# Moving ScalarE's division and beta k copy ahead of the silus of q and k in the first stage

## The chip, the core and the metric

The kernel runs on one NeuronCore of a Trainium2 chip. The metric is the device time of one execution in microseconds (us). The engines of the core are TensorE (PE in the profile; PEld is its weight load), VectorE (DVE), ScalarE (ACT), GpSimd (POOL) and SyncE (SP), which issues the DMAs. Each works through its own list of instructions in order and waits on semaphores for the others.

## The reference, cut to what matters

There are 32 samples of 750 x 256. Every second row is kept (384 tokens in three blocks of 128, the last padded), each block attends to itself, and a gated delta-rule attention and a mixture of six experts follow. Only the front of the second layer is touched by the change:

```python
h = _L0_tok_ref(x)                          # blockwise softmax attention
h = h + _L0_attn_ref(_layernorm(h), ...)
h = h + _L0_ffn_ref(_layernorm(h), ...)
# inside _L0_attn_ref
q = silu(causal_dwconv(x @ Wq, conv_q_w))   # 4 taps; k and v alike
beta = sigmoid(x @ Wb)
q = l2norm(q); k = l2norm(k)                # needs the sums of q*q and k*k by head
kb = k * beta[..., None]
A = tril(einsum('bhnid,bhnjd->bhnij', kbc, kc), -1)
```

All data is float32.

## The kernel before

The kernel has three stages. The first one, in `first_phase`, loads the samples and leaves q, k, v, beta k and the triangular systems in packs in DRAM. It is software-pipelined: each call of `body` works on three samples at once. For sample a it does the block attention and the layer norm statistics, for sample b the projections to q, k and v, the causal convolution and the silus of q and k, and for sample c the silu of v, the norms by head, the short filter, beta k and the product k (beta k). Every engine has a `body` of its own in which the calls for a, b and c are interleaved by hand, and that written order is the order in which the engine works. One turn of `body` is called a period below. There are 30 turns that hold all three samples, and a few at both ends that hold fewer.

The parts that the prediction follows, with the lines of the profile:

- TensorE: `attend` (L409) multiplies the probabilities by x and signals `attn_ready`. `transpose_kb` (L465) follows, then `project(b, ..., 5)` (L431, the last of six projections: two for q, two for k, two for v), then `k_kb` (L481, 96 small products of k and beta k, waiting for both halves of beta k). The next turn begins with `transpose_normed` (L417, waits for the normalised rows xn), `head_values` (L444, 36 matmuls of 128 columns; it waits for the squares of q and k through `sq_ready`), projections 0 and 1 (L431, waiting for both copies of the transposed xn) and `transpose_head_values` (L451).
- ScalarE: a tap of the convolution for each projection (`last_tap`, L579), the copy of the transposed probabilities and other copies (L541), the division of the attention rows by their sums (`divide_attn`, L563, three blocks), the silus (L588) and the squares SQ (L638). Silu and exp lie in different table sets, so each turn has two loads of a table (ACT_TABLE_LOAD), one at the first silu of q and one at the exp of beta (L573).
- VectorE: the other three taps of the convolution (L703), the copy of the second half of beta k (L775), the layer norm statistics (L670 to L676), the normalisation (L682, xn), the mask of the systems (L737), the second copy of the transposed xn (L687) and the short filter (L724, L728), which waits for the silus of v.
- GpSimd: the power that gives one over the standard deviation (L797), between L676 and L682.

The queue of SyncE stores the packs and loads the next sample in the same order of samples.

Of the kernel before, what the change touches and what calls it, by code (L numbers as in the profile page):

```python
# [146 lines left out]
def first_phase(nc, x, w, shared, v_all):  # L147

    NB, dram, bank, ident, upper, expanded = (shared[k] for k in ("NB", "dram", "bank", "ident", "upper", "expanded"))
    with ExitStack() as c:  # L150
# [5 lines left out]
        def signal(name, per=1, primed=1):  # L156
            signals.append(Signal(c.enter_context(nc.semaphore(name)), per, primed))
            return signals[-1]
# [38 lines left out]
        def field(buf, at):  # L197
            return buf[:, at:at + HALF * T]

        def chans(buf, at):  # L200
            return field(buf, at).rearrange("p (a t) -> p a t", a=HALF)

        def toks(buf, at):
            return field(buf, at).rearrange("p (b c) -> p b c", b=BLK)
# [3 lines left out]
        pack_stored = [signal(f"pack_stored{s}", 16) for s in range(2)]  # L208
# [57 lines left out]
        with nc.Block() as block:  # L266
            @block.vector
            def _(dve):
                dve.memset(wb[:, :, :], 0.0).then_inc(started, 1)
                dve.memset(headsel[:, :, :], 0.0).then_inc(started, 1)  # L270
                dve.wait_ge(started, 2)
                for n in range(2 * HALF):
                    for head in range(2):
                        dve.memset(headsel[head * DH:(head + 1) * DH, n, 2 * n + head:2 * n + head + 1], 1.0).then_inc(started, 1)
                dve.memset(minus_half[:, :], -0.5).then_inc(started, 1)
                for q in range(NQ):
                    dve.tensor_copy(strict[q * SC:(q + 1) * SC, :],
                                    upper[q * SC:(q + 1) * SC, P + q * SC:P + (q + 1) * SC]).then_inc(started, 1)
                dve.wait_ge(started, 11 + NQ)
# [30 lines left out]
        with nc.Block() as block:  # L310
# [227 lines left out]
            @block.scalar  # L538
            def _(act):
                def copy(dst, src):  # L540
                    return act.activation(dst, src, ACT.Copy)  # L541

                def copy_xT(n):
                    act.wait_ge(*xT_ready.now(n, 1))
                    copy(xT[:, 0:2, :, :].rearrange("p b a t -> p (b a t)"), bank[0][:, :]).then_inc(xT01_copied.sem, 1)

                def exp_scores(n):
                    act.wait_ge(*negmax_ready.now(n))
                    for b in range(BLK):
                        act.activation(E[:, b, :], bank[2][:, b * P:(b + 1) * P], ACT.Exp, bias=negmax[:, b:b + 1],  # L550
                                       scale=float(D) ** -0.5, accum_out=rs[:, b:b + 1]).then_inc(probs_ready.sem, 1)

                def copy_probsT(n):
                    act.wait_ge(*probsT_ready.now(n))
                    copy(PT[:, :, :].rearrange("p b t -> p (b t)"), bank[1][:, 0:T]).then_inc(probsT_copied.sem, 1)

                def divide_attn(n, s, pair):
                    H = toks(pb[s], HF)
                    act.wait_ge(*attn_ready.now(n))
                    act.wait_ge(*rinv_ready.now(n))  # L560
                    act.wait_ge(*h_stored[s].before(pair))
                    for b in range(BLK):
                        act.activation(H[:, b, :], attn_bank[b // 2][:, (b % 2) * D:(b % 2 + 1) * D], ACT.Copy,  # L563
                                       scale=rinv[:, b:b + 1]).then_inc(h_ready.sem, 1)

                def copy_xnT(n, s):
                    act.wait_ge(*xnT_ready.now(n, 1))
                    copy(chans(pb[s], XNT)[:, 0, :], bank[1][:, 0:T]).then_inc(xnT0_copied.sem, 1)

                def exp_beta(n):  # L570
                    act.wait_ge(*hvk_ready.now(n))
                    act.wait_ge(*beta_step.before(n))
                    act.activation(eb[:, :].rearrange("p (b h) -> p b h", b=BLK),  # L573
                                   hvk[:, :, 2 * NH:],
                                   ACT.Exp, scale=-1.0).then_inc(eb_ready.sem, 1)

                def last_tap(it, j):
                    act.wait_ge(*proj_ready.now(it, j + 1))
                    act.activation(Y[:, j, :], proj_bank[j][:, 0:T], ACT.Copy, scale=convw[:, j, CK - 1:CK])\  # L579
                        .then_inc(tap_done.sem, 1)  # L580

                def silu(it, s, j):
                    dst = (chans(pa[s], QT), chans(pa[s], KT), VT)[j // 2]
                    act.wait_ge(*conv_step.now(it, 6 * (j // 2) + 5 + j % 2))
                    if j == 4:
                        act.wait_ge(*fir_step.before(it))
                        act.wait_ge(*vtok_ready.before(it))
                    act.activation(dst[:, j % 2, :], Y[:, j, :], ACT.Silu).then_inc(silu_done.sem, 1)  # L588

                def body(a=None, b=None, c=None, s=0, apair=None, bpair=None):  # L590
                    if b is not None:
                        copy_xnT(b, 1 - s)
                    if c is not None:
                        silu(c, s, 4)
                        silu(c, s, 5)
                        act.wait_ge(*hv_ready.now(c))
                        copy(HVT[:, :], bank[6][0:BLK * SC, 0:P]).then_inc(hv_copied.sem, 1)
                    if b is not None:
                        last_tap(b, 0)
                        last_tap(b, 1)  # L600
                    if a is not None:
                        copy_xT(a)
                    if c is not None:
                        exp_beta(c)
                        act.wait_ge(*ktok_ready.now(c))
                        copy(field(pa[s], KTOK)[:, 0:2 * D], bank[6][:, :])
                        copy(field(pa[s], KTOK)[:, 2 * D:], bank[7][:, 0:D]).then_inc(ktok_copied.sem, 1)
                    if b is not None:
                        last_tap(b, 2)
                    if a is not None:  # L610
                        exp_scores(a)
                    if b is not None:
                        last_tap(b, 3)
                    if a is not None:
                        copy_probsT(a)
                    if c is not None:
                        act.wait_ge(*fs_ready.now(c))
                        act.wait_ge(*fs_stored.before(c))
                        copy(fsk[:, 0:2 * D], bank[6][:, :])
                        copy(fsk[:, 2 * D:], bank[7][:, 0:D]).then_inc(fs_copied.sem, 1)  # L620
                    if b is not None:
                        last_tap(b, 4)
                        act.wait_ge(*pack_stored[1 - s].before(bpair))
                        silu(b, 1 - s, 0)
                        silu(b, 1 - s, 1)
                    if a is not None:
                        divide_attn(a, s, apair)
                    if c is not None:
                        act.wait_ge(*kbT_ready.now(c, 1))
                        copy(chans(pa[s], KBT)[:, 0, :], bank[6][:, 0:T]).then_inc(kbT0_copied.sem, 1)  # L630
                    if b is not None:
                        silu(b, 1 - s, 2)
                        last_tap(b, 5)
                        silu(b, 1 - s, 3)
                        act.wait_ge(*silu_done.now(b, 4))
                        act.wait_ge(*ssq_ready.before(b))
                        for f in range(2):
                            act.activation(SQ[:, 2 * f:2 * f + 2, :].rearrange("p a t -> p (a t)"),  # L638
                                           field(pa[1 - s], (QT, KT)[f]), ACT.Square).then_inc(sq_ready.sem, 1)

                body(a=0, s=0, apair=0)
                body(a=1, b=0, s=1, apair=0, bpair=0)
                for i in range(0, NB // 2 - 1):
                    body(2 * i + 2, 2 * i + 1, 2 * i, 0, i + 1, i)
                    body(2 * i + 3, 2 * i + 2, 2 * i + 1, 1, i + 1, i + 1)
                body(b=NB - 1, c=NB - 2, s=0, bpair=NB // 2 - 1)
                body(c=NB - 1, s=1)
# [1471 lines left out]
```

## Time and profile before

| | us |
|---|---|
| median of 3 runs | 2776.16 |
| lowest, highest | 2775.27, 2777.48 |
| the profiled execution: device time | 2788.52 |
| the profiled execution: span of the trace | 2786.8 |
| first stage in the trace | about 0 to 770 |
| busy in the whole span: TensorE, VectorE, ScalarE, GpSimd | 2513.8, 1924.8, 1377.7, 537.1 |
| mean granted TensorE clock, share of full | 0.911 |

Times in the trace are read from the start of the span. A row of the view in order of time gives the start, the length, the engine, the line, the operation with output <- inputs, the shape and how many instructions are merged in it; behind it in brackets stands the time that the engine idled ahead of it and what ended that. The granted clock (PEclk) is 1.00 at 2.4 GHz and 0.50 at 1.2 GHz.

### The profile page before, as it was taken

The numbers are of one execution on the slowest core, as the hardware profiler recorded it, in microseconds if no ns is written. First come the engines' busy times: TensorE is split into PE (matmuls) and PEld (weight loads), VectorE is DVE, ScalarE is ACT, GpSimd is POOL, SyncE is SP. The second block draws the span as 40 slices with busy tenths as digits, with TensorE's granted clock in tenths as the row PEclk, the third lists the DMA queues.
The fourth block names the chain that finished last, engine by engine and source line by source line (L and its number), as shares of the span: only waits on it lengthen the run. The fifth ranks groups of instructions, "written<-read, shape, count | busy, mean of one in ns | idle before, by whom it ended". The sixth has DMA issues, their size and how long they took to land.

```text
span 2786.8 us, 53423 instructions
## 1 busy us (share of the span) xinstructions
PE 2513.8 (90%) x21052; PEld 1899.8 (68%) x21052; DVE 1924.8 (69%) x5233; ACT 1377.7 (49%) x2633; POOL 537.1 (19%) x373
## 2 busy tenths in 40 slices
PE   5888888888698789999999999999999999999997
PEld 3666666666477667777777777767777777677765
DVE  4888988898778245676667766776676566656655
ACT  3777777777533224444444454444444444444442
POOL 1333333333300011111111111111111111111110
PEclk9999999999896569999999999999899999999998
DMA  2666666666688411132123212221222122212200
GB/s 76 196 202 200 221 203 198 207 208 196 204 326 335 155 58 55 66 109 66 61 75 123 66 61 79 96 66 61 87 88 89 61 93 81 66 61 91 81 18 18
DMA packets 223161, 334.47 MB, mean 120 GB/s; under 512 B 113856, under 2 KB 190624, under 8 KB 213696
## 3 DMA queue, kind: packets, MB, share of 16 engines
q1 hardware_dynamic: 219744, 309.03, 33.6%
q10 hardware_dynamic: 2304, 12.58, 1.1%
q0 software_dynamic: 864, 9.44, 0.8%
q8 instruction: 168, 2.75, 0.4%
q14 instruction: 81, 0.66, 0.1%
HBM read 191.68 MB, written 164.23 MB: 128 GB/s over the span
## 4 chain that ended last, share of the span: by engine, by line
PE 49%; DVE 9%; ACT 6%; issue 3%; DVEq 0%
PE bank L1527 8%; PE bank L1537 8%; PE bank L1470 5%; PE bank L1365 4%; PE bank L1481 3%; PE bank L1499 3%; PE bank L1448 3%; ACT L1674 3%; PE bank L1433 2%; PE bank L1474 2%; PE bank L1396 2%; PE bank L1404 2%; DVE DL L1869 2%; DVE v_all L1955 1%; ACT HE L1674 1%
## 5 line engine op out<-in xcount | busy, mean ns | idle before, releaser
L1537 PE MATMUL bank<-w2e,HE 128*128 128x256 f32 x1152 | 312.4, 411 | 11.8 <-DVE v_all L1955 8.9
L1955 DVE SCALAR_TENSOR_TENSOR v_all<-bank,we,v_all 128x256 f32<-128x256 f32 x576 | 242.9, 477 | 111.1 <-PE bank L1537 108.8
L703 DVE SCALAR_TENSOR_TENSOR Y<-bank,convw,Y 128x383 f32<-128x383 f32 (+2 forms) x576 | 314.6, 606 | 5.9 <-ACT Y L579 5.9
L1527 PE MATMUL bank<-v_all,w1e 128*128 128x384 f32 x768 | 313.6, 535 | 1.3 <-ACT HE L1674 1.3
L431 PE MATMUL bank<-pb,wqkv 128*128 128x384 f32 x768 | 285.8, 503 | 6.6 <-issue 6.4
L1537 PEld LDWEIGHTS bank<-w2e,HE 128*128 128x128 f32 x1152 | 221.2, 203 | 53.5 <-issue 16.2
L1835 DVE TENSOR_TENSOR L<-bank,b2g 128x48 f32<-128x48 f32 x32 | 6.6, 207 | 342.3 <-PE bank L1481 342.3
L1674 ACT ACTIVATE HE<-bank 128x384 f32<-128x384 f32 x192 | 94.1, 490 | 222.4 <-PE bank L1527 221.7
L1470 PE MATMUL bank<-v_all,w1g 128*128 128x384 f32 x512 | 201.8, 517 | 0.4 <-ACT v_all L1666 0.4
L1527 PEld LDWEIGHTS bank<-v_all,w1e 128*128 128x128 f32 x768 | 146.7, 208 | 72.6 <-issue 23.3
L431 PEld LDWEIGHTS bank<-pb,wqkv 128*128 128x128 f32 x768 | 138.1, 197 | 79.9 <-issue 21.8
L803 POOL TENSOR_TENSOR RR<-RS,minus_half 128x24 f32<-128x24 f32 x32 | 133.2, 4163 | 273.8 <-DVE RS L752 273.8
L1657 ACT ACTIVATE v_all<-bank 128x192 f32<-128x192 f32 x192 | 60.2, 331 | 247.5 <-DVE v_all L1773 247.4
L2074 POOL TENSOR_TENSOR v_all<-v_all,WT 128x768 f32<-128x768 f32 x32 | 72.5, 2266 | 538.2 <-DVE WT L1854 538.2
L579 ACT ACTIVATE Y<-bank,convw 128x384 f32<-128x384 f32 x192 | 112.0, 584 | 77.1 <-PE bank L431 76.0
L2080 POOL TENSOR_TENSOR m<-m,minus_half_q 128x12 f32<-128x12 f32 x32 | 72.6, 2268 | 375.0 <-DVE m L1875 375.0
L1649 ACT ACTIVATE first_stage<-bank 32x384 f32<-32x384 f32 (+1 forms) x192 | 89.0, 479 | 98.8 <-PE bank L1385 43.1
L1448 PEld LDWEIGHTS bank<-W,v_all 128*128 128x128 f32 x768 | 107.6, 212 | 36.6 <-ACT W L1649 25.7
L1448 PE MATMUL bank<-W,v_all 128*128 128x64 f32 x768 | 113.6, 296 | 15.0 <-ACT W L1649 15.0
L1365 PE MATMUL bank<-v_all 64*128 64x256 f32 x768 | 116.4, 424 | 11.5 <-PEq L918 5.5
L1674 ACT ACT_TABLE_LOAD x93 | 119.3, 1283 | 1.8
L1470 PEld LDWEIGHTS bank<-v_all,w1g 128*128 128x128 f32 x512 | 87.9, 191 | 43.0 <-issue 1.2
(211 smaller groups left out, 5431.0 us busy)
## 6 DMA issues: line engine op xcount, KB each, us to landing
packa<-pa SPq DMA_DIRECT2D x32, 1932.0 KB, 8.1
v_all<-packa SPq DMA_DIRECT2D x32, 1932.0 KB, 7.7
packb<-pb SPq DMA_DIRECT2D x32, 768.0 KB, 6.1
v_all<-packb SPq DMA_DIRECT2D x32, 768.0 KB, 7.0
toeplitz<-taps SPq DMA_DIRECT2D x128, 190.0 KB, 5.1
toep<-toeplitz SPq DMA_DIRECT2D x32, 760.0 KB, 8.6
packb<-fsk SPq DMA_DIRECT2D x32, 384.0 KB, 2.3
first_stage<-fl SPq DMA_DIRECT2D x32, 384.0 KB, 5.4
```

Source lines behind the costliest of these rows:

```text
L431: mm = pe.matmul(proj_bank[j][:, 0:T], wqkv[:, a, j * P:(j + 1) * P], xnT[:, a, :], start=(a == 0), stop=(a == HALF - 1))
L579: act.activation(Y[:, j, :], proj_bank[j][:, 0:T], ACT.Copy, scale=convw[:, j, CK - 1:CK])\
L703: dve.scalar_tensor_tensor(out=Y[:, j, lag:T], in0=proj_bank[j][:, 0:T - lag], scalar=convw[:, j, CK - 1 - lag:CK - lag], in1=Y[:, j, lag: ...
L803: pool.tensor_tensor(RR[:, :, :, :].rearrange("p b n h -> p (b n h)"), RS[:, :], minus_half[:, :], ALU.pow)\
L1365: mm = pe.matmul(bank[odd][:, hh * 2 * P:(hh + 1) * 2 * P], kT[rows, hh, pair * P:(pair + 1) * P], qkb[rows, :, hh, pair * P:(pair + 1) * ...
L1448: mm = pe.matmul(bank[1][:, h * DH:(h + 1) * DH], ATM[:, even_heads_first(b, h), 0:P], W[:, h, :], start=(b == 0 and h == 0), stop=True, s ...
L1470: pe.matmul(mlp_bank[m][:, 0:T], w1g[:, a, m * P:(m + 1) * P], chans(pb[s], PX)[:, a, :], start=(a == 0), stop=False)
L1527: mm = pe.matmul(bank[6][:, 0:T], w1e[:, a, k, :], YT[s][:, a, :], start=(a == 0), stop=(a == HALF - 1))
L1537: mm = pe.matmul(expert_bank(b), HE[k % 2][:, b * P:(b + 1) * P], w2e[:, k, :], start=True, stop=True)
L1649: return act.activation(dst, src, ACT.Copy)
L1674: act.activation(HE[k % 2][:, :], bank[6][:, 0:T], ACT.Gelu_apprx_tanh).then_inc(he_ready.sem, 1)
L1955: dve.scalar_tensor_tensor(out=HA[s][:, b, :], in0=expert_bank(b), scalar=we[s][:, b, k:k + 1], in1=HA[s][:, b, :], op0=ALU.mult, op1=ALU. ...
```

## The change

In ScalarE's `body`, the silus of the two halves of q (`silu(b, 1 - s, 0)` and `1`) and the wait for the stored pack move behind the division of the attention rows of sample a and the copy of the first half of beta k of sample c. The last tap of the sixth projection (`last_tap(b, 5)`) moves ahead of all four silus. The number of instructions and of table loads stays the same.

```diff
                     if b is not None:
                         last_tap(b, 4)
-                        act.wait_ge(*pack_stored[1 - s].before(bpair))
-                        silu(b, 1 - s, 0)
-                        silu(b, 1 - s, 1)
                     if a is not None:
                         divide_attn(a, s, apair)
                     if c is not None:
                         act.wait_ge(*kbT_ready.now(c, 1))
                         copy(chans(pa[s], KBT)[:, 0, :], bank[6][:, 0:T]).then_inc(kbT0_copied.sem, 1)
                     if b is not None:
+                        last_tap(b, 5)
+                        act.wait_ge(*pack_stored[1 - s].before(bpair))
+                        silu(b, 1 - s, 0)
+                        silu(b, 1 - s, 1)
                         silu(b, 1 - s, 2)
-                        last_tap(b, 5)
                         silu(b, 1 - s, 3)
```

The lists of TensorE, VectorE, GpSimd and SyncE are the same in both programs. On ScalarE, in a turn with all three samples, from the tap of the fifth projection (L579, the row ahead of the table load) to the squares, there stands before:

```order
L579 ACTIVATE Y<-bank,convw 128x384
L588 ACT_TABLE_LOAD
L588 ACTIVATE pa<-Y 128x384 x2
L563 ACTIVATE pb<-bank,s 128x256 x3
L541 ACTIVATE pa<-bank 128x384
L588 ACTIVATE pa<-Y 128x384
L579 ACTIVATE Y<-bank,convw 128x384
L588 ACTIVATE pa<-Y 128x384
L638 ACTIVATE SQ<-pa 128x768 x2
```

and now:

```order
L579 ACTIVATE Y<-bank,convw 128x384
L563 ACTIVATE pb<-bank,s 128x256 x3
L541 ACTIVATE pa<-bank 128x384
L579 ACTIVATE Y<-bank,convw 128x384
L588 ACT_TABLE_LOAD
L588 ACTIVATE pa<-Y 128x384 x4
L638 ACTIVATE SQ<-pa 128x768 x2
```

The table load stands three kinds of work later, behind the division (L563), the copy of beta k (L541) and the tap of the sixth projection, and the four silus stand together between it and the squares.

On ScalarE in the last turn that has a sample b, and no sample a any more, there stands before, from the last copy of the short filter's rows on:

```order
L541 ACTIVATE fsk<-bank 128x256
L579 ACTIVATE Y<-bank,convw 128x384
L588 ACT_TABLE_LOAD
L588 ACTIVATE pa<-Y 128x384 x2
L541 ACTIVATE pa<-bank 128x384
L588 ACTIVATE pa<-Y 128x384
L579 ACTIVATE Y<-bank,convw 128x384
L588 ACTIVATE pa<-Y 128x384
L638 ACTIVATE SQ<-pa 128x768 x2
L588 ACTIVATE VT<-Y 128x384 x2
```

and now:

```order
L541 ACTIVATE fsk<-bank 128x256
L579 ACTIVATE Y<-bank,convw 128x384
L541 ACTIVATE pa<-bank 128x384
L579 ACTIVATE Y<-bank,convw 128x384
L588 ACT_TABLE_LOAD
L588 ACTIVATE pa<-Y 128x384 x4
L638 ACTIVATE SQ<-pa 128x768 x2
L588 ACTIVATE VT<-Y 128x384 x2
```

Here too the load stands behind the copy of beta k and the tap of the sixth projection.

## Rows read from the trace of the kernel before

**Rows 1.** Stretch: busy PE PEld DVE ACT POOL, PEclk, DMA, GB/s; four periods between silu table loads.
```profile
339.41:362.65 23.24, 20.38 (x216) 14.94 (x215) 19.58 (x52) 16.47 (x35) 8.05 (x7) 0.85 0.62 195
362.65:384.60 21.95, 19.05 (x216) 14.23 (x215) 19.63 (x52) 16.48 (x36) 8.05 (x7) 0.92 0.66 208
384.60:406.02 21.42, 17.75 (x216) 13.19 (x215) 19.57 (x52) 16.35 (x35) 8.04 (x7) 1.00 0.65 212
406.02:428.21 22.19, 19.34 (x216) 14.22 (x215) 19.62 (x52) 16.47 (x35) 8.11 (x8) 0.92 0.63 205
```

**Rows 2.** TensorE in order of time, in the period without low clock.
```profile
383.80 1.46 PE L409 MATMUL bank<-x,PT 128*128 128x256 f32 x6
...
385.75 1.46 PE L431 MATMUL bank<-pb,wqkv 128*128 128x384 f32 x4
388.39 1.01 PE L481 MATMUL bank<-pa 64*32 64x32 f32 x96 [1.19 <-issue]
391.07 0.88 PE L417 MATMUL bank<-ident,xn 128*128 128x128 f32 x6 [1.67 <-DVE xn L682]
391.88 1.07 PE L444 MATMUL bank<-SQ,headsel 128*32 128x128 f32 x24
392.78 0.61 PE L444 MATMUL bank<-pb,wb 128*32 128x128 f32 x12
394.20 2.82 PE L431 MATMUL bank<-pb,wqkv 128*128 128x384 f32 x8 [0.81 <-issue]
```

**Rows 3.** ScalarE in order of time, in the same period.
```profile
384.00 0.58 ACT L579 ACTIVATE Y<-bank,convw 128x384 f32<-128x384 f32 x1
384.60 1.28 ACT L588 ACT_TABLE_LOAD   x1
385.89 0.94 ACT L588 ACTIVATE pa<-Y 128x384 f32<-128x384 f32 x2
386.73 1.18 ACT L563 ACTIVATE pb<-bank,s 128x256 f32<-128x256 f32 x3
387.80 0.50 ACT L541 ACTIVATE pa<-bank 128x384 f32<-128x384 f32 x1
...
388.58 0.59 ACT L579 ACTIVATE Y<-bank,convw 128x384 f32<-128x384 f32 x1
389.05 0.54 ACT L588 ACTIVATE pa<-Y 128x384 f32<-128x384 f32 x1
389.62 1.58 ACT L638 ACTIVATE SQ<-pa 128x768 f32<-128x768 f32 x2
```

**Rows 4.** VectorE in order of time, in the same period.
```profile
385.95 0.56 DVE L775 COPY pa<-bank 128x384 f32<-128x384 f32 x1 [0.64 <-PE bank L465]
387.22 1.16 DVE L670 BATCH_NORM_STATS2 st<-pb 128x6 f32<-128x256 f32 x3 [0.72 <-ACT pb L563]
...
389.96 1.06 DVE L682 TENSOR_SCALAR xn<-pb,mv,s 128x256 f32<-128x256 f32 x3
...
393.56 0.55 DVE L687 COPY pb<-bank 128x384 f32<-128x384 f32 x1
```

**Rows 5.** TensorE in order of time, in the last turn with a sample b.
```profile
745.03 1.07 PE L444 MATMUL bank<-SQ,headsel 128*32 128x128 f32 x24 [1.84 <-ACT SQ L638]
```

**Rows 6.** TensorE in order of time, in the period with 6.83 us at low clock.
```profile
347.36 1.93 PE L444 MATMUL bank<-SQ,headsel 128*32 128x128 f32 x24
...
350.07 3.58 PE L431 MATMUL bank<-pb,wqkv 128*128 128x384 f32 x8
```

**Rows 7.** The same view as rows 1, the stretches at low clock.
```profile
344.74:351.57 6.83, 5.68 (x45) 4.13 (x46) 6.70 (x17) 3.08 (x6) 0.00 (x0) 0.50 0.91 300
368.63:372.05 3.42, 2.88 (x27) 2.42 (x30) 3.42 (x9) 1.91 (x4) 0.00 (x0) 0.50 0.91 364
...
413.00:416.42 3.42, 3.42 (x41) 2.48 (x40) 3.30 (x8) 1.59 (x4) 0.00 (x0) 0.50 0.89 274
```

**Rows 8.** Silu's table load in the first stage: count, length, first and last start.
```profile
L588 ACT ACT_TABLE_LOAD  x30: 1283/1283/1283, 73.1 to 719.1; - x30
```

## The prediction

> **What bounds the kernel now.** I read the busy times by period first. All 30 full turns lie between the silu table loads from 73.1 to 719.1 us [rows 8], so a period is (719.1 - 73.1) / 29 = 22.28 us. The four shown come in turn: 23.24, 21.95, 21.42 and 22.19 us, at a mean granted clock of 0.85, 0.92, 1.00 and 0.92 [rows 1]. The order of instructions is the same in all four, and ScalarE and VectorE are busy for the same time in each; only TensorE's clock differs. So the period has two parts: a base of 21.42 us at full clock, and what the low clock adds.
>
> The base is read from the orders in time of the period at full clock. Zero is 384.60, where the table load starts [rows 3]. TensorE has three gaps: 1.19 us ahead of the products of k and beta k, 1.67 us ahead of the transposes of xn (VectorE), and 0.81 us ahead of projection 0 [rows 2], which starts when VectorE has copied its half of the transposed xn at 393.56 + 0.55 = 394.11 [rows 4]. Elsewhere it runs through. The first gap waits for ScalarE's copy of beta k, which ends at 388.30 [rows 3]; the second is the chain division, statistics, xn, in which VectorE idles 0.72 us for ScalarE's division [rows 4]. That is what the change goes for.
>
> **The low clock.** It is granted at 344.74 for 6.83 us, at 368.63 for 3.42 us, not at all in the third period, and at 413.00 for 3.42 us [rows 1, 7]. Against the zero of its own period it starts at +5.33, +5.98 and +6.98. All three starts lie behind the first gaps of TensorE. In the stretch of 6.83 us TensorE was idle for 6.83 - 5.68 = 1.15 us before it ran on; in the two of 3.42 us for 0.54 us and not at all [rows 7].
>
> **The change, on ScalarE.** The attention product ends at 383.80 + 1.46 = 385.26 [rows 2]. ScalarE is free at 384.60, and now waits 0.70 us, which the table load used to fill. Then, with the distances of start to start in [rows 3]:
> - division at 385.30, not 386.73;
> - copy of beta k 1.07 later, at 386.37, done at 386.87, not 388.30;
> - tap of the sixth projection, which ends at 385.75 + 1.46 = 387.21 [rows 2]: at 387.26, not 388.58. ScalarE waits 0.5 us here as well;
> - table load 0.60 later, at 387.86; first silu 1.29 later, at 389.15; the fourth three times 0.42 later, at 390.41 (0.84 for two); squares 0.57 later, at 390.98, not 389.62; done at 392.56, not 391.20.
>
> **On VectorE.** Its copy of beta k stays at 385.95 to 386.51, since that waits for TensorE. The statistics start at 386.53 instead of 387.22, 0.69 us earlier, and the chain through GpSimd to xn moves by the same, so xn starts at 389.27 instead of 389.96 [rows 4]. The second copy of the transposed xn then ends near 393.42 instead of 394.11. The short filter, next, waits for the silus of v, which ScalarE ends near 394.0; it stays within the slack that projection 0 leaves.
>
> **On TensorE.** The products of k and beta k start at 387.25: the gap of 1.19 us is gone. They take 1.01 us, and then it waits until 391.07 - 0.69 = 390.38 for the transposes of xn: a gap of 2.1 us instead of 1.67. Those end at about 391.2. Then comes what is new: head_values needs the squares, and starts at 392.56 + 0.05 = 392.61 instead of 391.88, after a gap of 1.4 us. That it can wait for them the last turn shows, where TensorE idles 1.84 us for the squares already [rows 5]. From 391.88 to 393.39 less the 0.07 by which neighbouring groups overlap it takes 1.44 us [rows 2], so projection 0 starts at 394.05 instead of 394.20. The rest of the turn is TensorE's own as before. The base becomes 21.42 - 0.15 = 21.27 us: of 1.4 us gained at the division, 0.15 is left, since the squares are 1.36 us later.
>
> **What the clock adds now.** Before, 0.81 us of slack ahead of projection 0 swallowed part of each low stretch. Now head_values has none behind it. At low clock it takes 350.07 - 347.36 = 2.71 us [rows 6] instead of 1.44: +1.27. Eight matmuls of projection took 3.58 us with the first 1.50 us at low clock, against 2.82: 0.76 lost, half the low time [rows 2, 6, 7]. In the changed period head_values starts at +8.01 (392.61) and ends at +10.72 at low clock. A low stretch of 6.83 us that starts at +X therefore costs 1.27 + (X + 6.83 - 10.72) / 2.
>
> Which stretch comes is the choice on which the forecast rests. TensorE is idle from +3.7 to +5.8 and from +6.6 to +8.0, with 0.8 us of transposes between. I take it that the clock falls in every period, since the two gaps together (3.5 us) are nearly as long as the three of before (3.67 us) but stand closer, and that it stays low for 6.83 us: the second gap, 1.4 us, lies in the first part of a stretch that begins between +5.3 and +6.6, as the 1.15 us did in the long stretch of before. For X the rows give a hint. After the period of 23.24 us with the long stretch the next start came 5.98 - 5.33 = 0.65 us later in its period [rows 1, 7]; a period of 23.24 + 0.65 = 23.89 us would find it in the same place. X = 6.6 gives 1.27 + 1.36 = 2.63 and 21.27 + 2.63 = 23.90 us, so this place reproduces itself: a start earlier than that makes the period shorter and moves the next start later. The bounds are X = 5.3 (+1.98, period 23.25) and X = 7.1 (+2.88, 24.15).
>
> **The sum.** 29 periods x (23.90 - 22.28) = +47.0 us; about -1 until the start has settled; in the last turn TensorE waits for the squares already, so their 1.4 us come on top: +47. With the bounds +28 and +54. The second and third stage have the same instructions. The trace has 2786.8 us of span in 2788.52 of device time; I add the difference to the median: 2776.2 + 47 = 2823 us. Its own range is 2804 to 2832.
>
> **A rule of the skill.** The rows show low clock after gaps of 1.19 and 1.67 us [rows 2, 7]. The Trainium skill, page "TensorE: Matmul & The Clock Gate", section "HAM oscillation — how this bites in real kernels", tells of a loop whose matmuls wait for a DMA in each K-tile, 3 to 5 us long, and that paid the low clock in every turn. If only gaps that long cost the clock, this kernel's would be free and the result that of rival three; the rows contradict that, as three of four periods pay.
>
> **Rivals.**
> One, a short stretch in each period: after the fall the clock is full again 3.42 us later. It would start between +7.3 and +8.9, and cost 1.27 to 1.66, so 22.5 to 22.9 us a period: +8 to +20 us, 2784 to 2796. For it speaks that two of three stretches of before were short; against it the second gap.
> Two, the pattern of before stays (5.33 long, 5.98 short, none, 6.98 short). Then the four periods are 23.26, 21.92, 21.27 and 22.40, with 1.38 and 2.41 us of head_values at low clock at 1.27 / 2.71 each. They sum to 88.85 against 88.80: no change, 2776 to 2780. Against it: one of the four now has a gap of 1.4 us where it had none.
> Three, faster: TensorE's first gap is closed, and if that is what let the clock fall, no period has a low stretch. Then 29 x (21.27 - 22.28) = -29 us, 2749. The point is whether 2.1 us and 1.4 us of idleness with work between keep the clock; the third period had 1.67 and 0.81 and kept it. I hold it for unlikely, as the gaps grow.
> Four, the low stretch grows longer than 6.83 us, or the squares are later than worked out (another 0.5 us a period is +15 us): 2835 to 2860.
> That the change doesn't act can be left out: the division did wait behind the load [rows 3].
>
> **Chances.** The forecast 0.55, rival one 0.17, two 0.12, three 0.08, four 0.08. A measurement of this kernel can tell 0.2% (5.6 us) from no change, so slower is 0.80, same 0.12, faster 0.08. The range leaves out rival three and most of two and four: 2778 to 2836 us.
>
> **What would show it.** In the trace after: division about 1.4 us earlier against the tap ahead of it; TensorE's gap ahead of the products of k and beta k gone, that ahead of the transposes of xn near 2.1 us, and a wait of head_values for the squares of about 1.4 us in nearly every turn; a period of 23.9 us with a mean clock of (23.9 - 3.42) / 23.9 = 0.86 against 0.92 now. If head_values does not wait for the squares, the step on ScalarE is wrong; if the base at full clock is not near 21.3, the path; if base and gaps are right and the period isn't, the clock.

## The result and the profile after

The changed kernel takes 2828.88 us (median of 4 runs, 2824.33 to 2839.04) against 2776.82 us (2775.27 to 2779.96) before: a ratio of 1.0191, with a 95% interval of 1.0162 to 1.022. It is slower by 52 us, 1.9%, clear of the noise. The prediction said 2823.

Two turns of the changed kernel in the view of busy time by stretch, from silu table load to load, and the low stretches of three turns with the full one between them; columns as in [rows 1]:

```profile
410.24:434.13 23.89, 20.36 (x237) 14.73 (x227) 19.41 (x52) 16.37 (x36) 8.05 (x6) 0.86 0.58 190
434.13:458.02 23.89, 20.36 (x237) 14.72 (x226) 19.41 (x53) 16.37 (x35) 8.06 (x6) 0.86 0.59 191
437.51:444.34 6.83, 5.50 (x41) 3.67 (x42) 4.86 (x10) 2.76 (x6) 0.00 (x0) 0.50 0.88 232
444.34:461.40 17.06, 14.87 (x175) 11.05 (x173) 14.55 (x42) 13.61 (x30) 8.06 (x6) 1.00 0.47 175
461.40:468.23 6.83, 5.49 (x41) 3.67 (x42) 4.86 (x10) 2.76 (x6) 0.00 (x0) 0.50 0.82 221
```

These answer [rows 1] and [rows 7]. The four different periods of before (23.24, 21.95, 21.42, 22.19 us) have become one, 23.89 us, with a low stretch (half clock, PEclk 0.50) of 6.83 us in each. The table loads, by count, length, first and last start:

```profile
L588 ACT ACT_TABLE_LOAD  x30: 1283/1283/1283, 76.5 to 768.6; - x30
```

(768.6 - 76.5) / 29 = 23.87 us against 22.28 [rows 8]. TensorE in order of time through one turn; it answers [rows 2] and [rows 6]:

```profile
432.03 1.46 PE L431 MATMUL bank<-pb,wqkv 128*128 128x384 f32 x4
433.42 1.02 PE L481 MATMUL bank<-pa 64*32 64x32 f32 x96
436.48 0.87 PE L417 MATMUL bank<-ident,xn 128*128 128x128 f32 x6 [2.04 <-DVE xn L682]
438.84 1.93 PE L444 MATMUL bank<-SQ,headsel 128*32 128x128 f32 x24 [1.49 <-ACT SQ L638]
440.55 1.07 PE L444 MATMUL bank<-pb,wb 128*32 128x128 f32 x12
441.55 4.22 PE L431 MATMUL bank<-pb,wqkv 128*128 128x384 f32 x8
```

The gap ahead of the products of k and beta k (L481) is gone. The one ahead of the transposes of xn has grown from 1.67 to 2.04 us, and head_values (L444) now waits 1.49 us for the squares. It then runs at low clock for 441.55 - 438.84 = 2.71 us, and the eight matmuls of projection behind it take 4.22 us instead of 2.82. ScalarE and VectorE in order of time in the same turn, which answer [rows 3] and [rows 4]:

```profile
431.58 1.20 ACT L563 ACTIVATE pb<-bank,s 128x256 f32<-128x256 f32 x3 [0.71 <-PE bank L409]
432.67 0.50 ACT L541 ACTIVATE pa<-bank 128x384 f32<-128x384 f32 x1
433.53 0.58 ACT L579 ACTIVATE Y<-bank,convw 128x384 f32<-128x384 f32 x1 [0.36 <-PE bank L431]
434.13 1.28 ACT L588 ACT_TABLE_LOAD   x1
435.42 1.76 ACT L588 ACTIVATE pa<-Y 128x384 f32<-128x384 f32 x4
437.22 1.58 ACT L638 ACTIVATE SQ<-pa 128x768 f32<-128x768 f32 x2
```
```profile
432.71 1.07 DVE L670 BATCH_NORM_STATS2 st<-pb 128x6 f32<-128x256 f32 x3
435.37 1.06 DVE L682 TENSOR_SCALAR xn<-pb,mv,s 128x256 f32<-128x256 f32 x3
438.96 0.55 DVE L687 COPY pb<-bank 128x384 f32<-128x384 f32 x1
440.03 0.75 DVE L724 TENSOR_SCALAR fsT<-VT,firw 128x384 f32<-128x384 f32 x2 [0.52 <-ACT VT L588]
```

ScalarE idles 0.71 us for the attention product and 0.36 us for the sixth projection, time in which the table load and silus used to run. VectorE no longer waits for the division. Its statistics follow its copy of beta k at once.

### The profile page after: what moved, and what is told of

Same layout as the page of the kernel before. It is cut to its first block, busy times and chain, and to the rows that moved or that the text cites. A ratio compares the mean times of both kernels' runs of the same rounds, so it can differ in the third digit from the quotient of the medians.

```text
span 2828.5 us, 53423 instructions
## 1 busy us (share of the span) xinstructions
PE 2538.6 (90%) x21052; PEld 1904.4 (67%) x21052; DVE 1920.4 (68%) x5233; ACT 1375.9 (49%) x2633; POOL 537.5 (19%) x373
## 4 chain that ended last, share of the span: by engine, by line
PE 46%; DVE 11%; ACT 6%; issue 3%; DVEq 0%
PE bank L1537 8%; PE bank L1527 7%; PE bank L1470 5%; PE bank L1365 4%; PE bank L1481 3%; PE bank L1499 3%; ACT L1674 3%; PE bank L1448 2%; PE bank L1474 2%; PE bank L1433 2%; DVE DL L1869 2%; PE bank L1396 2%; PE bank L1404 2%; DVE v_all L1955 2%; ACT HE L1674 1%
## 5 line engine op out<-in xcount | busy, mean ns | idle before, releaser
L431 PE MATMUL bank<-pb,wqkv 128*128 128x384 f32 x768 | 320.3, 553 | 0.9 <-issue 0.7
L431 PEld LDWEIGHTS bank<-pb,wqkv 128*128 128x128 f32 x768 | 154.9, 220 | 94.2 <-issue 49.9
L579 ACT ACTIVATE Y<-bank,convw 128x384 f32<-128x384 f32 x192 | 111.8, 582 | 122.4 <-PE bank L431 121.2
```

What stands on the lines that cost most here:

```text
L431: mm = pe.matmul(proj_bank[j][:, 0:T], wqkv[:, a, j * P:(j + 1) * P], xnT[:, a, :], start=(a == 0), stop=(a == HALF - 1))
```

## The experiments

In every kernel below "period" is the distance of the silu table loads: last start less first start, by 29. Ratios are to the kernel before in the same set of runs.

### Filling the gaps, first size (e1, e2)

To tell a loss by the clock from a loss by the wait, the order is left alone and TensorE is given work in its gaps. The work is without use and its result is overwritten; such matmuls are called fillers below. The clock theory says that the 52 us are the low clock; the path rival says that they are the new wait of TensorE for the squares.

```diff
+                def fill(n, k):
+                    for _ in range(n):
+                        pe.matmul(bank[k][:, 0:P], ident[:, :], ident[:, :], start=True, stop=True, skip_group_check=True)
...
+                        fill(14, 1)             # e1; e2: fill(11, 1)
                         transpose_normed(b)
...
+                        pe.wait_ge(*at_copied.before(c))
+                        fill(9, 6)              # e1 alone
                         head_values(c, s)
...
+                        fill(8, 1)              # e2 alone
                         k_kb(c, s)
```

> The changed kernel, with idle TensorE time filled: in each full turn 14 matmuls of the identity by itself (128 columns, about 0.13 us each) ahead of the wait for xn, and 9 ahead of the wait for the squares, into banks that are free there; their results are overwritten. Clock theory (the loss is the low clock that every turn takes on behind the gaps, the path itself is about 0.1 us a turn shorter than before): no low stretch is left in the full turns, the period is 21.3 us, the time 2748 us (2742 to 2756). Path rival (the loss is the wait for the squares itself): the fillers only sit in gaps, the period stays at 23.9 us and the time near 2829 us. If only one of the gaps matters, something between.

> The kernel before, with 8 such matmuls ahead of the products of k and beta k and 11 ahead of the wait for xn. Clock theory: no low stretch, every period as the one at full clock, 21.4 us, so 2776 - 29 x 0.86 = 2751 us. Path rival: 2776 us. The difference to the filled changed kernel is the path alone: clock theory says that kernel is the faster one by 2 to 5 us, path rival slower by some 50.

Measured: e1 2796.13 us, ratio 1.0065 (1.0042 to 1.0088), period 22.78 us; e2 2770.68 us, ratio 0.9966 (0.9945 to 0.9987), period 21.87 us. Neither theory's number came. Busy time by stretch of e1, and its fillers on TensorE in order of time:

```profile
300.00:500.00 200.00, 200.00 (x2318) 162.15 (x2317) 169.93 (x445) 143.74 (x304) 69.51 (x51) 1.00 0.63 205
```
```profile
394.25 3.39 PE L489 MATMUL bank<-ident 128*128 128x128 f32 x28
397.48 0.82 PE L417 MATMUL bank<-ident,xn 128*128 128x128 f32 x6
398.14 2.17 PE L489 MATMUL bank<-ident 128*128 128x128 f32 x18
400.24 1.07 PE L444 MATMUL bank<-SQ,headsel 128*32 128x128 f32 x24
```

### Filling the gaps, right size (e5, e6, e8, e11)

The same edit with 8 and 5 fillers in the changed kernel (e5), 4 and 6 in the kernel before (e6), and in the changed kernel one gap alone: 8 fillers ahead of xn (e8), 5 ahead of the squares (e11).

> The changed kernel with shorter fillers: 8 matmuls of the identity ahead of the wait for xn and 5 ahead of the wait for the squares. One takes 0.23 us in the trace of e1, so they make 1.9 and 1.2 us and fit into the gaps of 2.04 and 1.49 us, where those of e1 (3.2 and 2.1 us) were longer than the gaps. Clock theory: full clock in every turn, period 21.3 us, 2776 - 29 x 1.0 = 2747 us, give or take 8 for the later stages. Path rival: not below 2776, since the changed path has a wait more.

> The kernel before with fillers that fit its gaps: 4 (0.9 us) ahead of the products of k and beta k, 6 (1.4 us) ahead of the wait for xn. Clock theory: every turn as the one at full clock, 21.42 us, 2776 - 29 x 0.86 = 2751 us, give or take 8; e5 is then 0.15 us a turn, 4 us, faster than this. Path rival: e5 is the slower of the two.

> The changed kernel with the gap ahead of xn filled alone (8 fillers), that of 1.4 us ahead of the squares left. If the gap ahead of xn lets the clock fall and the second only keeps it low, every turn is at full clock and the period 21.3 us, 2747 us. If the gap for the squares is enough by itself, there are low stretches in some or all turns and the time lies between 2760 and 2829 us.

> The changed kernel with only the gap ahead of the squares filled (5 fillers), that of 2.04 us ahead of xn left. If the gap ahead of xn lets the clock fall and the gap for the squares keeps it low, there are low stretches again but only short ones (3.4 us): 21.3 to 22.6 us a turn, 2750 to 2785 us. If the gap ahead of xn keeps the clock low by itself, the period stays at 23.9 us and the time at 2829 us.

| kernel | median us | ratio (95%) | period us |
|---|---|---|---|
| e5 changed, both gaps | 2756.48 | 0.9907 (0.9881 to 0.9932) | 21.26 |
| e6 before, both gaps | 2757.27 | 0.9922 (0.9899 to 0.9945) | 21.45 |
| e8 changed, gap ahead of xn alone | 2748.78 | 0.9889 (0.9861 to 0.9916) | 21.26 |
| e11 changed, gap ahead of the squares alone | 2765.58 | 0.9942 (0.9925 to 0.996) | 21.66 |

Table loads of e5, e6, e8 and e11, in that order:

```profile
L597 ACT ACT_TABLE_LOAD  x30: 1283/1283/1283, 75.3 to 691.9; - x30
```
```profile
L596 ACT ACT_TABLE_LOAD  x30: 1283/1283/1283, 73.0 to 695.1; - x30
```
```profile
L594 ACT ACT_TABLE_LOAD  x30: 1283/1283/1283, 76.2 to 692.6; - x30
```
```profile
L595 ACT ACT_TABLE_LOAD  x30: 1283/1283/1283, 77.4 to 705.6; - x30
```

The stretch from 300 to 500 us of e8, and TensorE in one of its turns:

```profile
300.00:500.00 200.00, 186.12 (x2125) 142.36 (x2124) 182.73 (x481) 154.06 (x335) 78.23 (x59) 1.00 0.65 211
```
```profile
397.39 0.87 PE L417 MATMUL bank<-ident,xn 128*128 128x128 f32 x6
399.76 1.07 PE L444 MATMUL bank<-SQ,headsel 128*32 128x128 f32 x24 [1.50 <-ACT SQ L644]
```

Here the wait for the squares is whole, 1.50 us, the clock is full, and the period is 21.26 us, 1.0 us less than the 22.28 of the kernel before, and 0.19 less than that kernel with its own gaps filled (e6). So the wait alone costs nothing net: the changed path is the shorter one. What costs is the clock: with the gap of 2.04 us ahead of xn filled, there is no low stretch in any full turn (nor in those of e5 and e6). With only the other filled (e11), every second or third turn has a low stretch, and it is short. The turn of e11 that holds one, the inner part of the stretch, and the full clock behind it until after the next load; then TensorE in that turn:

```profile
402.02:424.43 22.41, 20.37 (x248) 15.64 (x237) 19.42 (x53) 16.38 (x35) 8.06 (x6) 0.92 0.61 204
405.60:408.80 3.20, 3.20 (x34) 2.80 (x36) 2.69 (x7) 2.29 (x5) 0.00 (x0) 0.50 0.84 205
409.00:427.80 18.80, 16.76 (x193) 12.45 (x188) 16.32 (x46) 13.88 (x31) 8.06 (x6) 1.00 0.55 196
```
```profile
404.37 0.88 PE L417 MATMUL bank<-ident,xn 128*128 128x128 f32 x6 [2.04 <-DVE xn L689]
405.09 1.96 PE L489 MATMUL bank<-ident 128*128 128x128 f32 x10
406.98 1.93 PE L444 MATMUL bank<-SQ,headsel 128*32 128x128 f32 x24
```

TensorE goes from the transposes to head_values without a wait, and the clock is back after some 3.4 us. So the gap ahead of xn can bring the low clock by itself, in 10 of the 29 periods of e11, the gap of 1.5 us for the squares by itself does not (e8), and the long stretch in every turn came only with both.

The medians of e5, e6 and e8 differ less clearly than the periods. e5 and e8 have the same first stage and stand 8 us apart, which lies in the later stages and between executions. e5 came 1.5 us above its range of 2739 to 2755, and its median is only 0.8 us below that of e6 where 4 us were expected, which the noise hides. So both medians refute the path rival, which wanted e5 not below 2776, but that the changed path is shorter rests on the periods, 21.26 against 21.45 us.

### More work, same period (e3, e9)

Two fillers are added where TensorE runs without a gap, to the changed kernel (e3) and to the kernel before (e9):

```diff
                     pe.wait_ge(*xnT1_copied.before(n))
+                    fill(2, 0)
                     for b in range(BLK):
                         for a in range(HALF):
```

> The changed kernel with 2 more matmuls of 128 columns (0.27 us) in each turn ahead of the transposes of x, where TensorE runs without a gap and sets the pace. Self-reproducing theory: the period stays at 23.89 us, since the low stretch begins some 0.5 us earlier in its turn and costs 0.27 us less: 2829 us, within 3. Additive rival: 31 x 0.27 = 8 us more, 2837 us, low stretches in place.

> The kernel before with 2 more matmuls of 128 columns in each turn ahead of the transposes of x (0.47 us a turn, at the 0.23 us that one took in e1). Self-reproducing theory: 21.43 + 0.47 = 21.9 us at full clock; the long low stretch of before, starting at +5.3 to +5.7, cost 1.8 to 1.95 us, and 21.9 + 1.95 comes near 23.89 us, so the turns fall into step with the low stretch and stay there: 23.9 us a turn, 2776 + 47 = 2823 us, for 14 us of added work. Additive rival: 2776 + 14 = 2790 us, with the four alternating periods each 0.47 us longer.

Measured: e3 2829.49 us, ratio 1.0186 (1.013 to 1.0241), against 2828.88 for the changed kernel without them. At 0.23 us each the two add 0.47 us a turn, not 0.27, so the additive rival should have given 14 us. e9: 2828.44 us, ratio 1.0162 (1.0099 to 1.0225), 47 us for some 14 us of work. One turn of e3 and a part of its low stretch, then the same of e9:

```profile
438.20:462.09 23.89, 20.97 (x242) 15.45 (x231) 19.40 (x53) 16.43 (x35) 8.05 (x6) 0.86 0.57 192
440.80:447.40 6.60, 5.72 (x45) 4.10 (x44) 5.63 (x12) 3.51 (x8) 0.00 (x0) 0.50 0.81 240
```
```profile
494.69:518.58 23.89, 21.03 (x220) 15.54 (x219) 19.58 (x52) 16.53 (x35) 8.04 (x7) 0.86 0.59 190
500.60:507.20 6.60, 6.03 (x45) 4.43 (x46) 6.46 (x15) 2.50 (x5) 0.00 (x0) 0.50 0.85 272
```

In e3 the low stretch begins 440.7 - 438.2 = 2.5 us after the table load, where in the changed kernel it is 437.51 - 434.13 = 3.38 us. It begins some 0.9 us earlier in its turn, and with half the low time lost that gives back the 0.47 us. So a later low stretch costs more and an earlier one less, and the turn settles where both agree.

The changed kernel itself shows how. The first of its 29 periods and the low stretch in it:

```profile
76.51:100.02 23.51, 20.43 (x238) 14.82 (x228) 19.41 (x53) 16.38 (x36) 8.07 (x6) 0.85 0.60 194
79.11:85.94 6.83, 5.79 (x45) 3.95 (x44) 5.63 (x12) 3.51 (x8) 0.00 (x0) 0.50 0.93 269
```

The next long stretch starts at 103.00, 23.89 us after this one, though the period took 23.51. The same distance stands in the kernel before, 368.63 - 344.74, across a period of 23.24 us [rows 7]. A period that is shorter than 23.89 us therefore finds the next stretch later in its turn by what is missing, and half of that is added to the next period. The first periods are 23.51, 23.70, 23.79, 23.85 and 23.87 us: what is missing to 23.89 halves each time. Why long stretches stand 23.89 us apart, no run here shows.

e9 has the order of before, without the change, and reaches the same 23.89 us. It did not do so at once: its first eight periods varied between 21.9 and 24.8 us, so that its mean is 23.52, and its runs spread from 2804 to 2843.

### One part undone (e4)

The tap of the sixth projection goes back between the third and fourth silu; division and copy of beta k stay ahead.

```diff
-                        last_tap(b, 5)
                         act.wait_ge(*pack_stored[1 - s].before(bpair))
                         silu(b, 1 - s, 0)
                         silu(b, 1 - s, 1)
                         silu(b, 1 - s, 2)
+                        last_tap(b, 5)
                         silu(b, 1 - s, 3)
```

> The changed kernel with one part undone: the tap of the sixth projection stands between the third and fourth silu as before; division and copy of beta k stay ahead of the silus. The squares end 0.66 us earlier than in the changed kernel, but VectorE's first taps of v wait for the late tap, and xn and the second copy of the transposed xn come 1.1 us later: base 21.8 us, the gap ahead of the transposes of xn 3.2 us. Clock theory: one low stretch in every turn, period 22.6 to 23.9 us, 2786 to 2823 us, and no wait for the squares. Path rival (the wait for the squares is the loss): the time falls to that of before or below, 2770 to 2785 us.

Measured: 2831.9 us, ratio 1.0187 (1.0141 to 1.0234); period 23.84 us, and 23.89 a turn once settled, with the time 9 us above the range I gave. TensorE in order of time:

```profile
433.10 1.02 PE L481 MATMUL bank<-pa 64*32 64x32 f32 x96
437.64 1.54 PE L417 MATMUL bank<-ident,xn 128*128 128x128 f32 x6 [3.52 <-DVE xn L682]
439.11 1.93 PE L444 MATMUL bank<-SQ,headsel 128*32 128x128 f32 x24
```

There is no wait for the squares, and the kernel is as slow. The two waits are one wait of 3.52 us now, and the low stretch is again 6.83 us in every settled turn. This speaks against the path rival a second time, though less than e8 does, since TensorE idles as long in sum as before (3.53 us). It also shows that the long stretch does not need a second gap: one gap of 3.52 us brings it too.

### One silu ahead of the division (e7, e10)

The table load can fill ScalarE's wait for the attention product without holding up the division, if only one silu goes with it.

```diff
                         last_tap(b, 4)
+                        act.wait_ge(*pack_stored[1 - s].before(bpair))
+                        silu(b, 1 - s, 0)
                     if a is not None:
                         divide_attn(a, s, apair)
...
                         last_tap(b, 5)
-                        act.wait_ge(*pack_stored[1 - s].before(bpair))
-                        silu(b, 1 - s, 0)
                         silu(b, 1 - s, 1)
```

e10 is this alone; e7 has 2 fillers ahead of the products of k and beta k and 6 ahead of the transposes of xn besides.

> An order between the two: one silu of q stays ahead of the division, so that the table load fills ScalarE's wait for the attention product; the other three stand behind the tap of the sixth projection as in the changed kernel; 2 and 6 fillers ahead of the products of k and beta k and of the wait for xn. From the same rows: division 1.71 us after the fifth tap (2.13 before, 0.70 in the changed kernel), squares done at 6.61 (6.60, 7.96), xn 0.42 us earlier than before, no wait for the squares, projection 0 at 9.18 instead of 9.60: period 21.0 us, 2776 - 29 x 1.28 = 2739 us, give or take 8. If something else sets the pace at full clock, the period is 21.3 or more and the time 2747 or more.

> The order of e7 (one silu of q ahead of the division, three behind the tap of the sixth projection) without fillers. At full clock 21.02 us a turn (e7), with gaps of 0.7, 1.75 and 0.9 us. 23.89 us is out of reach: the long stretch would have to cost 2.87 us. So low stretches come in some turns as in the kernel before: 21.5 to 22.2 us a turn, 2754 to 2774 us. Rival (any ordering that is faster at full clock falls into step at 23.89 us as the changed kernel did): 2823 us or more.

Measured: e7 2741.32 us, ratio 0.986 (0.9833 to 0.9886), period 21.03 us; e10 2757.92 us, ratio 0.9916 (0.9884 to 0.9948), period 21.34 us, a little below the range of 21.5 to 22.2, while the time is within its range. Table loads and a stretch of e7, then of e10:

```profile
L596 ACT ACT_TABLE_LOAD  x30: 1283/1283/1283, 71.1 to 681.0; - x30
300.00:500.00 200.00, 188.01 (x2248) 145.05 (x2245) 186.23 (x486) 156.57 (x333) 76.43 (x59) 1.00 0.66 217
```
```profile
L588 ACT ACT_TABLE_LOAD  x30: 1283/1283/1283, 73.9 to 692.7; - x30
300.00:500.00 200.00, 172.21 (x1982) 128.28 (x1982) 185.16 (x482) 155.31 (x333) 79.58 (x59) 0.98 0.66 214
```

Both beat the two kernels. e10 does it by order alone: more than half of its turns take 21.02 us, and the others, most of them with a short low stretch of 3.4 us, 21.5 to 22.1. So a path that is faster at full clock need not fall into step. The expectation gives a reason, that a long stretch would have to cost 2.87 us to reach 23.89; that this is what keeps e10 out is argued and not tested.

## Why the prediction was right, point by point

- **ScalarE's chain.** The forecast counts from where the table load stood before, 0.60 us behind the start of the fifth tap. In the trace after, the tap of the next turn starts at 454.18, so that point is 454.78, and a turn of 23.89 us earlier 430.89. The division starts at +0.69, the load at +3.24 (forecast 3.26), the squares end at 437.22 + 1.58 = 438.80, +7.91 (7.96).
- **VectorE's chain.** xn starts at +4.48; forecast 389.27 - 384.60 = +4.67. The statistics start at +1.82 (forecast +1.93) and take 1.07 us where they took 1.16 while the division gated them. The forecast was 0.2 us late here, and for the turn it does not matter, since TensorE waits for the squares behind it.
- **TensorE's gaps.** Forecast: none, 2.1 and 1.4 us. Measured: none, 2.04 and 1.49.
- **The base at full clock.** Forecast 21.27 us; e5 and e8 show 21.26, and e6 shows 21.45 for the order before, where the prediction had read 21.42. The path gained 0.19 us a turn, about what was said (0.15).
- **The low clock.** A stretch of 6.83 us in every turn was the choice on which the forecast rested. It starts at 437.51 - 430.89 = +6.62; the forecast was +6.6. head_values takes 2.71 us in it, as taken over from [rows 6], and the turn is 23.89 us against 23.90. The reason given for the place, that a start earlier than that makes the turn shorter and moves the next start later, is what e3 and the first periods of the changed kernel show. The first low stretch starts at 79.11, which is 79.11 - (76.51 - 3.24) = +5.84, and the rule of the prediction gives 21.26 + 1.27 + (5.84 + 6.83 - 10.72) / 2 = 23.51 us, the measured period. The reason given for the length, the second gap, fits e11, which takes that gap away; e4 shows that one longer gap does the same. That the clock falls in every turn was taken from the sum of the gaps. It came so, but no run tests that reason by itself, and the prediction gave its whole forecast only 0.55.
- **The sum.** 29 x (23.87 - 22.28) = 46.1 us, against 47 - 1. What was mis-sized is the end of the stage. The sum put 1.4 us there. The last transposes of head values (L451) came 798.79 - 747.08 = 51.7 us later than before. Measured from the point where the table load stood before, 0.2 us of this lies ahead of the 29 periods and 5.4 us behind them. About 2.5 us of the 5.4 is the thirtieth turn with its low stretch, which a sum over 29 distances leaves out. The other 2.9 us is the last turn: head_values starts 1.9 us later in it, as the squares keep TensorE 4.40 us instead of 1.84 [rows 5] and only a part of that was won ahead of them, and a low stretch that begins at 795.94, behind this gap, makes head_values and what follows up to L451 take 3.08 us instead of 2.05.

ScalarE's fifth tap in the turn behind the one shown; TensorE in the last turns of the changed kernel, with the low stretch there; and the row of the kernel before that answers TensorE's last one:

```profile
454.18 0.58 ACT L579 ACTIVATE Y<-bank,convw 128x384 f32<-128x384 f32 x1
```
```profile
780.12 0.25 PE L451 MATMUL bank<-ident,HVT 96*128 96x96 f32 x1
...
795.71 1.76 PE L444 MATMUL bank<-SQ,headsel 128*32 128x128 f32 x24 [4.40 <-ACT SQ L638]
...
798.79 0.39 PE L451 MATMUL bank<-ident,HVT 96*128 96x96 f32 x1 [0.46 <-ACT HVT L541]
```
```profile
795.94:799.36 3.42, 2.78 (x37) 2.05 (x31) 2.84 (x7) 1.52 (x4) 0.00 (x0) 0.50 0.82 194
```
```profile
747.08 0.27 PE L451 MATMUL bank<-ident,HVT 96*128 96x96 f32 x1 [0.55 <-ACT HVT L541]
```

- **The rivals.** A short stretch in each turn did not come, nor the pattern of before, nor a longer stretch. The faster case named its condition well, that the clock stays full, and e8 and e5 show what it would have brought: 2749 and 2756 us, against the 2749 worked out.
- **The rule of the Trainium skill.** Gaps of 2.04 and 1.49 us brought the low clock in every turn of the changed kernel. The Trainium skill, page "TensorE: Matmul & The Clock Gate", section "HAM oscillation — how this bites in real kernels", has an example whose waits are 3 to 5 us long, and both gaps here are shorter. The example is right in kind, that a loop can pay in each turn; its length is no limit below which a gap is free.

What stays open: why the clock falls in every turn of the changed kernel and in three of four before; why executions of one kernel differ (the kernel before from 2763 to 2794 us beside e1), which blurs comparisons of medians that stand a few us apart. In the profiled executions of the kernel before and the changed one the span grew by 2828.5 - 2786.8 = 41.7 us, though the first stage grew by 51.7; the remaining 10 us lie behind it and were not followed.

## What to carry to other kernels

When an edit shortens a chain but moves where an engine idles, work out TensorE's gaps of the new order and price its clock, not the path alone: here the path gained 0.2 us a turn and the clock took 1.8 us more than before. Before work is moved out of a wait in one engine's list, look what filled it: a table load in front of a wait costs less by as much as it overlaps the wait, and behind the wait all of it is on the chain. And where TensorE has idle time that can't be closed, a few matmuls of no use in it, sized to fit the gap, can be worth as much as a good reordering: in the order of before they brought a ratio of 0.9922 (e6), the best reordering alone 0.9916 (e10), both together 0.986 (e7).

## What the runs showed of the hardware that was not expected

- Turns of different work come out at the same length, the distance at which long low stretches follow each other. The changed kernel, the same with 0.47 us more work, the one with the late tap and the kernel before with 0.47 us more all settled at 23.89 us, with bases at full clock of 21.26 (e5), and, as estimated from e5, the expectation of e4 and e6, of 21.7, 21.8 and 21.9 us. In that state neither a small gain nor a small loss in TensorE's work shows in the time.
- The other side of it: 0.47 us of work a turn in the kernel before, 14 us in all, cost 47 us.
- A float32 product of 128 columns by the identity takes 0.23 us where a transpose of the same shape takes 0.13.
